# TensorE's transposes of T move to VectorE; operands of two blocks in one instruction; whole batches loaded in quarters

## What is computed

```python
# x: (8, 512, 512), T: (100, 512, 512), itok: (8,) in 1..98, all matrices fp32
Tb = T[itok - 1]
return x + jnp.einsum('bij,bjk->bik', Tb, x)
```

## Time and profile before

| | us |
|---|---|
| median of 3 timed runs | 116.84 |
| lowest, highest | 116.51, 118.35 |
| span of the profiled execution | 117.3 |
| PE busy in it | 108.4 (92%) |
| DVE busy | 96.2 (82%) |
| POOL busy | 81.2 (69%) |
| ACT busy | 67.0 (57%) |
| mean rate of the DMAs | 215 GB/s |

### The profile page before, as it was taken

How to read it: one execution, slowest core, us unless ns; L and a number is a source line. 1 busy time by engine, 2 the same in 40 slices (tenths; PEclk the granted TensorE clock), 3 DMA queues, 4 the chain that set the end, 5 groups by cost and what they waited for, 6 DMA issues and landing times. The chain is left out here.

```text
span 117.3 us, 1986 instructions
## 1 busy us (share of the span) xinstructions
PE 108.4 (92%) x512; PEld 89.9 (77%) x512; DVE 96.2 (82%) x139; ACT 67.0 (57%) x125; POOL 81.2 (69%) x68
## 2 busy tenths in 40 slices
PE   4945999999799999999999999999999999999990
PEld 4925888888588877888888888887788878777880
DVE  0196769999946999999978999799989996899681
ACT  2715499658129958458277853995098624933000
POOL 2364587996738957996788876895789586874400
PEclk9996799999999999999999999999999999999999
DMA  2799974448887895447998599749982897222233
GB/s 86 231 310 255 344 205 147 129 105 294 229 296 254 279 320 194 153 124 238 287 257 291 157 293 363 229 122 298 353 242 92 256 278 281 87 89 89 103 133 122
DMA packets 15416, 25.26 MB, mean 215 GB/s; under 512 B 1712, under 2 KB 6064, under 8 KB 15408
## 3 DMA queue, kind: packets, MB, share of 16 engines
q1 hardware_dynamic: 14976, 24.39, 66.6%
q10 hardware_dynamic: 432, 0.79, 2.0%
HBM read 16.78 MB, written 8.39 MB: 215 GB/s over the span
## 5 line engine op out<-in xcount | busy, mean ns | idle before, releaser
L249 POOL TENSOR_TENSOR TD_r<-TH_r,TL 128x512 fp32r<-128x512 f32 x32 | 42.3, 1323 | 21.3 <-DVE TL L290 21.2
L243 POOL TENSOR_TENSOR xL<-x_sb,xH 128x512 fp32r<-128x512 f32 x30 | 39.2, 1308 | 7.1 <-ACT xH L191 7.1
L382 PE MATMUL same<-xH,TH_r 128*128 128x512 f32 x124 | 36.5, 417 | 0.4 <-DVE out_sb L315 0.3
L412 PE MATMUL diff<-xD,TD_r 128*128 128x512 f32 x128 | 34.3, 391 | 0.0
L389 PE MATMUL same<-xL,TL 128*128 128x512 f32 x124 | 33.4, 391 | 0.0
L191 ACT ACTIVATE xH<-x_sb 128x512 fp32r<-128x512 f32 x32 | 20.3, 634 | 22.5 <-DMA x_sb<-x 19.6
L412 PEld LDWEIGHTS diff<-xD,TD_r 128*128 128x128 f32 x128 | 24.0, 188 | 5.0
L389 PEld LDWEIGHTS same<-xL,TL 128*128 128x128 f32 x124 | 23.4, 189 | 5.4
L382 PEld LDWEIGHTS same<-xH,TH_r 128*128 128x128 f32 x124 | 22.0, 195 | 5.2 <-DVE out_sb L315 1.8
L315 DVE SCALAR_TENSOR_TENSOR out_sb<-same,rest 128x512 f32<-128x512 f32 (+1 forms) x33 | 22.3, 676 | 2.9 <-PE same L404 0.2
L290 DVE TENSOR_TENSOR TL<-turned_ps,TH 128x512 fp32r<-128x512 f32 x24 | 16.2, 677 | 8.6 <-ACT TH L199 8.5
(11 more groups left out here) (15 smaller groups left out, 22.6 us busy)
## 6 DMA issues: line engine op xcount, KB each, us to landing
out<-out_sb SPq DMA_DIRECT2D x31, 256.0 KB, 3.8
x_sb<-x SPq DMA_DIRECT2D x29, 256.0 KB, 4.6
T_sb<-T SPq DMA_DIRECT2D x7, 768.0 KB, 5.1
T_cols_sb<-T SPq DMA_DIRECT2D x32, 64.0 KB, 4.1
x_sb<-x ACTq DMA_DIRECT2D x3, 256.0 KB, 3.5
T_sb<-T SPq DMA_DIRECT2D x3, 256.0 KB, 6.3
out<-out_sb SPq DMA_DIRECT2D x2, 128.0 KB, 1.9
```

The lines of the kernel that those rows point to most:

```text
L243: nc.gpsimd.tensor_tensor(xL[s][:, n], x_sb[s][:, n], xH[s][:, n].bitcast(fp32), ALU.subtract).then_inc(done, 1)
L249: nc.gpsimd.tensor_tensor(TD_r[n][:], TH_r[n][:].bitcast(fp32), TL[n][:].bitcast(fp32), ALU.subtract).then_inc(TD_ready, 1)
L382: nc.tensor.matmul(same[n % 2][:], TH_r[n][:, j], xH[s][:, j], start=(j == 0), stop=False)
L412: done = nc.tensor.matmul(diff[n % 2][:], TD_r[n][:, j], xD[s][:, j], start=(j == 0), stop=(j == N - 1))
```

## The change

- VectorE turns every block of T (line 284 of the new kernel), from loads in runs of 512 bytes, reading 32 consecutive elements at a time, into a pair of PSUM banks `turned` that holds two blocks. TensorE turns nothing.
- x, out and the contraction are laid out as `(g u c)` on the partitions, so x, T and out are moved by four DMAs of 32 partitions each (`load_x`, `load_T`, `store`), 256 KB per DMA. x has 4 slots, T 2, out 2; the block-wise stores and loads become one group per batch.
- The operands are made for two blocks in one instruction (128x1024): TH_r, TL, TD_r, and the three parts of x. TH is no longer made: TL = turned - 4096 TH_r. The sets of operands grow (3 of x, 4 pairs of T). xH_copy is one pair of banks.
- The output is still made by rest and out_sb, block by block.
- The loop over batches is unrolled; the last block of the last batch isn't split any more.
- In a step k (two blocks) VectorE runs: two transposes of pair k+2, the sum of block 2k-1, TL of pair k+2, the sum of block 2k, xD of half k+3 (a half is two of a batch's four quarters of x).

Core of the diff (SyncE's loop over batches, ScalarE's loop over steps, the transpose, VectorE's loop over steps):

```diff
-    S = 2
-    AHEAD = 2
-    BY_DVE = N - 1
+    UNITS = B * N
+    PAIRS = UNITS // 2
+    X_SLOTS, T_SLOTS, X_SETS, T_SETS, OUT_SLOTS = 4, 2, 3, 4, 2
-    x_rows = x.rearrange("b (p n) k -> b p n k", n=N)
-    T_rows = T.rearrange("t (p n) j -> t p n j", n=N)
-    T_cols = T.rearrange("t (m q n) (g c) -> t n g q m c", q=Q, n=N, g=G)
+    x_part = x.rearrange("b (g u c) k -> b g c u k", g=G, c=Q)
+    T_part = T.rearrange("t (m n q) (g c) -> t g q m n c", n=N, q=Q, g=G)
...
+            for b in range(B):
+                if b + T_SLOTS < B:
+                    t = matrix(b + T_SLOTS)
+                    sp.wait_ge(turned_ready, (b + 1) * N)
+                    for g in range(G):
+                        load_T(t, b + T_SLOTS, g)
+                if b < B - 1:
+                    sp.wait_ge(sum_ready, (b + 1) * N)
+                    for g in range(G):
+                        store(sp, b, g, slice(0, N), stored[b % OUT_SLOTS])
+                    if b + X_SLOTS < B:
+                        for g in range(G):
+                            load_x(sp, b + X_SLOTS, g)
...
+            for k in range(PAIRS):
+                for p in T_pairs(k)[:1]:
+                    cut_T_pair(p)
+                for h in x_halves(k)[:1]:
+                    cut_x_half(h)
+                for h in x_halves(k)[:1]:
+                    copy_xH_half(h)
...
-                nc.vector.transpose(turned_sb[:].rearrange("p j (m q) -> p m j q", q=Q),
-                                    T_cols_sb[s][:].rearrange("p m (c j) -> p m j c", j=N)
-                                    ).then_inc(turned_by_dve, 1)
+                nc.vector.transpose(turned[:, U % 2].rearrange("p u (m q) -> p m u q", q=Q),
+                                    rows.rearrange("p m (u c) -> p m u c", c=Q)).then_inc(turned_ready, 1)
...
+            for k in range(PAIRS):
+                for p in T_pairs(k)[:1]:
+                    turn(2 * p)
+                    turn(2 * p + 1)
+                if k:
+                    sum_up(2 * k - 1)
+                for p in T_pairs(k)[:1]:
+                    cut_T_pair(p)
+                sum_up(2 * k)
+                for h in x_halves(k)[:1]:
+                    cut_x_half(h)
...
```

More of the change, by code:

```diff
@@ L92, in cond_resid, with T_pairs, x_halves, half @@
         same_ready = sem("same_ready")
+        rest_ready = sem("rest_ready")
         diff_ready = sem("diff_ready")
-        rest_ready = sem("rest_ready")
         sum_ready = sem("sum_ready")
-        stored = [sem(f"stored{n}") for n in range(N)]
+        stored = [sem(f"stored{s}") for s in range(OUT_SLOTS)]
+        last_stored = sem("last_stored")
         block = ctx.enter_context(nc.Block())
[L99 to L129, removed]
+        def T_pairs(k):
+            return [p for p in ([1, 2] if k == 0 else [k + 2]) if p < PAIRS]
+        def x_halves(k):
+            return [h for h in ([2, 3] if k == 0 else [k + 3]) if h < 2 * B]
+        def half(tiles, h):
+            return tiles[h // 2 % X_SETS][:, 2 * (h % 2):2 * (h % 2) + 2]
+        def load_x(eng, b, g):
+            s = b % X_SLOTS
+            eng.dma_start(x_sb[s][g * Q:(g + 1) * Q], x_part[b, g]).then_inc(x_loaded[s], 16)
+        def store(eng, b, g, tiles, done):
+            eng.dma_start(out_part[b, g, :, tiles], out_sb[b % OUT_SLOTS][g * Q:(g + 1) * Q, tiles]).then_inc(done, 16)
         @block.sync
@@ L233, in _ @@
+            act.wait_ge(sum_ready, UNITS)
+            for g in range(G // 2, G):
+                store(act, B - 1, g, slice(N - 1, N), last_stored)
         @block.gpsimd
@@ L347, in _ @@
+            sum_up(UNITS - 1)
         @block.tensor
         def _(pe):
-            def warm_up(times):
-                for _ in range(times):
-                    nc.tensor.matmul(diff[1][:, 0:P], eye[:], eye[:], start=True, stop=True)
-            def turn(s, n):
-                rows = T_sb[s][:, n].rearrange("p (c j) -> p j c", j=N)
-                for j in range(N):
-                    done = nc.tensor.transpose(turned[n][:, j], rows[:, j], eye[:])
-                done.then_inc(turned_by_pe, 1)
@@ L377, in multiply_same, with warm_up @@
-            def multiply_same(b, s, n, first):
-                pe.wait_ge(TH_ready, b * N + n + 1)
+            def warm_up():
+                for _ in range(WARM):
+                    nc.tensor.matmul(same[1][:, 0:P], eye[:], eye[:], start=True, stop=True)
+            def multiply_same(U):
+                b, n = U // N, U % N
+                p, i, s = U // 2 % T_SETS, U % 2, b % X_SETS
+                if U >= 2:
+                    pe.wait_ge(sum_ready, U - 1)
+                pe.wait_ge(TH_ready, U + 1)
```

396 lines of the change are left out of this document (182 added, 214 removed).

## The result

The changed kernel takes 160.44 us (median of 4 runs, 159.48 to 160.54) against 117.59 for the kernel before in the same comparison: 1.373 times as long, interval 1.366 to 1.380. Some executions of the kernel before fall into a slower state (up to 120.97 us here), so the ratios compare only the fast executions of both kernels. The forecast was slower, 137.0 us, with a range up to 152; the sign holds, the size doesn't. The profiled execution took 160.41 us, its span is 158.6.

What follows compares the result with a forecast made beforehand. A loop over four engines, GpSimd's pair weighing most, was to bound: 28.8 start + 12 x 7.05 + 4.0 waits for T, then 2.6, 13.6, 1.4 and 2.5 gave 137.5 span, 137.0 us timed; range 126 to 152.

Steps and rivals of the forecast that it cites:

- start of step 13 to the end: After the twelve steps: transposes and block 25's sum 2.6, TensorE's five blocks 13.6, last sum 1.4, store 2.5.
- The step's chain: Per two-block step: transposes, TH_r, cut of x, xL, xD and handoffs, about 7.05 us; VectorE waits 0.85 before xD.
- step 0: First step, two steps of T and x with only one sum: 14.1 us, so step 1 begins at 28.8.
- The loads of T: SyncE's T loads behind a batch's sum: last quarter lands at 15.0, wanted at 14.1; wait 1.0 for four batches, 4.0.
- Are through by then: 2.1 MB of out and x ahead of T, at 290 GB/s, are moved before T's last quarter lands at 15.0.
- the zero: Start of the step in which a batch's last sum falls, from which the times of T's loads are counted.
- rival 3: Quarter loads are slow: at half of 290 GB/s a batch takes 21.7 us, total 158; at 189 GB/s 16.7, near 150; chance 0.11.
- The start: Before step 0: VectorE's first transpose at 6.8 us after T lands, two xD 1.7, its opening work through at 14.7.
- Rival 4: TensorE still bounds, not slower than before: 104 us if steps come under 5.44, break-even step some 5.9; chance 0.06.
- The end: After TensorE's last blocks at 133.6: last sum 1.4 and its store 2.5, span 137.5, timed median 0.4% below.
- TensorE's clock: At the lower clock level a block would take 5.4 us and a step 10.9; expected to come back, counted as nothing.

Runs made afterwards that it cites:

- cut_x_first: Changed kernel with ScalarE cutting the half of x ahead of the pair's TH_r; 158.36 us.
- T_first_cut_x_first: Changed kernel with index and loads of T ahead of the wait for the sum and stores, and the cut of x ahead of TH_r; 129.49 us.
- full_moves: Changed kernel with x and out (but the last batch's) moved by DMAs of 128 partitions, T still in quarters, product of permuted rows; 154.43 us.
- T_before_x: Changed kernel with SyncE's order per batch stores, index and T, x instead of stores, x, index and T; 145.53 us.
- index_early: Changed kernel with only the read of the next index moved ahead of the wait for the sum; 159.06 us.
- T_first: Changed kernel with SyncE's index and loads of T for batch b+3 ahead of the wait for batch b's sum; 142.04 us.
- full_index_early: Changed kernel with x and out in DMAs of 128 partitions and the index read early, permuted rows; fastest 152.27 us, other three 155.17 to 155.69.

## Why the prediction was wrong in size and right in kind

The prediction's sum, in terms of span, against what the timeline shows:

| | predicted | measured |
|---|---|---|
| start of step 1 | 28.8 | 32.59 |
| 12 steps | 84.6 | 86.1 (7.12 to 7.23 each) |
| waits for T | 4.0 | 18.1 |
| start of step 13 to the end | 20.1 | 21.85 (136.75 to 158.6) |
| span | 137.5 | 158.6 |

**The step's chain: right.** All links stand in order, 7.12 for 7.05, with VectorE's wait of 0.96 on average (0.86 in the twelve steps after step 0) for 0.85. cut_x_first and T_first_cut_x_first undid it and got VectorE's own sum, 6.18 for the 6.20 worked out. Of the unseen prices, the transpose (0.60 taken, 0.61 by distances), VectorE's pair (1.13, measured 1.14) and GpSimd's (2.5, measured 2.39) were near.

**The loads of T: the step that failed.** "Eight issues of 0.46 ... lands 4.1 later ... I take a wait of 1.0" came to 4.1 to 5.1. The links were named, and undersized: eight issues took 6.0 to 7.2, not 3.7. Stores and loads of x in the timeline, in the batch where they were shortest (the longest is shown above):

```profile
42.35 2.81 SPq L97 DMA_DIRECT2D out<-out_sb  x4
45.20 3.16 SPq L94 DMA_DIRECT2D x_sb<-x  x4
```

A store from 32 partitions takes 0.70 to issue where one of 128 takes 0.46 (1.84 for four in full_moves). A load of x to 32 partitions takes 0.79 to 1.09 right behind such stores, but 0.48 behind loads of T (1.91 for four in T_before_x): what stands ahead of it weighs more than its 32 partitions. The price of 0.46 was from loads at the start, with no stores ahead. The last quarter of T, 256 KB in 512-byte runs, lands 5.1 after its issue, not the 4.1 of a 64 KB one. "Are through by then" held only because T was issued late: out and x moved at 230 GB/s, not 290, until about 89 us, 12 after the zero, and at the 10.9 of the prediction they would still have been moving. So the drain fills about the same time as the issues, and index_early, which cut the issues alone, gained 1.4 us. In the batch shown, the last quarter went out at 14.3 after the zero, not 10.9, and landed at 19.4, not 15.0. The range was too narrow at this term (0 to 10, against 18.1), though rival 3 held the slow quarters.

**Rival 3: its rate in part, its consequence not.** It put the time at 158 from a rate halved, with DMAs as the bound; that this is close to 160 is luck. The rate is down by a quarter from the 290 assumed, a batch takes neither the 21.7 nor the 16.7 us of that rival, and T_first shows that the DMAs don't bind: the same moves in another order give 142.04. The order is what is needed for the waits: without it the quarters leave none (T_first), and with it, x and out in full DMAs still leave 12.0 of the 18.1 us (full_moves). The quarters add the rest, by longer issues as well as slower moves; the split between these two stays open (full_moves changed both, and full_index_early decided nothing).

**The start: 3.8 us late.** The first transpose began at 8.73, not 6.8: its loads landed 3.7 after the last was issued, where I had taken 2, the lower end, although has 4.1 for loads of this kind. And the xD beside GpSimd's xL (both operands in SBUF) cost 1.73 each, not 0.85:

```profile
8.73 0.73 DVE L284 STREAM_TRANSPOSE turned<-first_T 128x512 f32<-128x512 f32 x1 [8.73 <-DMA first_T<-T]
...
10.68 2.95 POOL L218 TENSOR_TENSOR xL<-x_sb,xH 128x512 fp32r<-128x512 f32 x2 [1.25 <-ACT xH L157]
10.72 3.46 DVE L263 SCALAR_TENSOR_TENSOR xD<-xL,xH 128x512 fp32r<-128x512 f32 x2
...
18.37 1.30 DVE L284 STREAM_TRANSPOSE turned<-T_sb 128x512 f32<-128x512 f32 x2
```

Step 0 itself, 18.37 to 32.59, is 14.2 for 14.1 (its terms add up to 14.0). Rival 4's break-even, a step of some 5.9, was too high by the same start: T_first_cut_x_first has 6.20 and takes 129.5, 12.6 over the 116.84 of the kernel before, so twelve steps would have to be near 5.15 (an estimate from these numbers).

**The end:** the last store took 3.8 us, from 154.76 to 158.6, not 2.5. And the timed run lies 1.8 above its span, where I had set it 0.5 below, by mixing the span of one execution with the median of others: 2.3 us of the miss.

**TensorE's clock: counted at nothing, rightly.** It was at the lower level for part of many stretches after waits for T; one stretch behind such a wait (columns as the earlier trace rows):

```profile
80.00:90.00 10.00, 10.00 (x34) 8.00 (x35) 8.40 (x11) 4.53 (x5) 6.95 (x3) 0.74 0.91 208
```

TensorE is busy throughout at a mean grant of 0.74, between its two levels. VectorE waited 6.0 us in all for `diff`, 5.8 of it over the last blocks, where nothing but TensorE's number of blocks is left to bound. The block that starts at 79.80 takes 5.29 us instead of 2.72, and the step around it 7.13 (77.13 to 84.26), no more than the others. The slack that TensorE has in a step hides the clock.

## What to carry to other kernels

An order of issues that waits for a batch's last result ahead of the next batch's loads closes a loop through the queue: write down the loop's links and compare them with the period before believing any engine's sum, and put the loads that are needed first ahead of stores and of loads that have slots to spare. A DMA of 32 partitions is priced from a row of its own kind, for its rate and, if it is a store, for its issue; a load's issue depends more on what stands ahead of it in the queue. When a chain inside a step is cut while a longer loop outside it holds, little comes of it: cut_x_first gave 2 us alone and 12.5 on top of T_first.

## What the runs showed of the hardware

- VectorE pays 0.37 us per 512 fp32 elements for reading every fourth one, in a scalar_tensor_tensor (0.69 to 1.05) as in a transpose (0.73 to 1.09), and 0.19 in a copy. The transpose takes fp32 at the pace of the other instructions, to PSUM (727 ns) as to SBUF (711).
- Moves of 32 partitions against 128: loads 203 against 276 GB/s, stores 234 against 311, as means of groups of 4.2 MB; inside the groups 221 against 329 to 400, and 261 against 369. Loads and stores in quarters mixed in one queue carried 251 GB/s.
- A 32-partition load of 256 KB took SyncE 0.48 us to issue behind loads and 0.79 to 1.09 behind 32-partition stores (T_before_x against the changed kernel).
- Two SBUF operands on VectorE beside GpSimd's tensor_tensor slow each other: xD 1.73 us each and xL 1.48, where GpSimd otherwise takes 1.31 and an xL of VectorE, also with two SBUF operands, took 0.67 while GpSimd stood idle (at 9.36 us).
